# Running the first four attention slots inside the feed-forward stage of a two-layer transformer kernel

## The reference

```python
xn = _layernorm(x)
x = x + attn(xn, w_qkv, w_o) + ffn(xn, w_fc, w_proj)
# attn: 32 query heads, 4 key/value heads of 64, rotary embedding on q and k,
#       causal softmax over 256 keys, output projection from 2048 to 256
# ffn:  layer_norm, absmax quantisation (a straight-through value), ternary weights,
#       256 -> 1024, gelu, the same again, 1024 -> 256
```

## Time and profile before

| | us |
|---|---|
| median of 3 runs | 435.03 |
| lowest and highest run | 432.61, 436.24 |
| profiled execution | 434.22 |
| its span | 432.4 |
| PE busy | 394.3 (91%) |
| DVE busy | 359.2 (83%) |
| POOL busy | 279.6 (65%) |
| ACT busy | 264.0 (61%) |
| TensorE clock granted, mean | 0.976 |

### The profile page before, as it was taken

One profiled execution on the slowest core, in us unless ns is written; L12 is line 12 of the kernel. 1 busy time (PEld: TensorE's weight loads), 2 busy tenths in 40 slices (PEclk: granted clock), 3 DMA queues, 4 the chain that ended last, 5 costly groups with the idle time before them and its releaser, 6 DMA issues.

```text
span 432.4 us, 8674 instructions
## 1 busy us (share of the span) xinstructions
PE 394.3 (91%) x3002; PEld 362.9 (84%) x3002; DVE 359.2 (83%) x696; ACT 264.0 (61%) x818; POOL 279.6 (65%) x206
## 2 busy tenths in 40 slices
PE   3869796899978999999999989999998999999895
PEld 2556775699868999899999989999998999999785
DVE  3759699887738999889888987988998998899983
ACT  3350338877446667567666756766664676766671
POOL 6300152005879589986969998696998959697400
PEclk9977989999996999999999999999999999999999
DMA  7992040002453435543433554343346524324400
GB/s 230 375 349 72 0 181 15 2 1 50 108 130 81 99 76 130 133 98 72 107 92 85 131 130 122 74 104 93 90 115 145 133 48 116 86 64 113 106 2 24
DMA packets 39437, 45.20 MB, mean 105 GB/s; under 512 B 5601, under 2 KB 31970, under 8 KB 39138
## 3 DMA queue, kind: packets, MB, share of 16 engines
q1 hardware_dynamic: 39248, 44.65, 39.6%
q10 hardware_dynamic: 146, 0.00, 0.0%
HBM read 13.18 MB, written 1.05 MB: 33 GB/s over the span
## 4 chain that ended last, share of the span: by engine, by line
PE 43%; POOL 18%; DVE 17%; SPq 8%; issue 6%; ACT 4%; DMA 4%; POOLq 0%; ACTq 0%
PE bank L1273 7%; PE bank L1240 7%; PE bank L964 6%; PE bank L1291 6%; PE bank L1149 6%; DVE prob L916 5%; SPq L388 4%; POOL rope_a L627 4%; POOL split_hi L637 4%; POOL rope_a L638 4%; POOL rope_b L629 4%; POOL split_lo L639 3%; PE bank L1022 2%; DMA qT<-split_lo 2%; DVE neg_max L902 2%
## 5 line engine op out<-in xcount | busy, mean ns | idle before, releaser
L916 DVE TENSOR_TENSOR prob<-prob,rsum 128x512 f32<-128x512 f32 x96 | 112.5, 1172 | 3.3
L554 ACT ACTIVATE prob<-bank,neg_max 128x256 f32<-128x256 f32 (+1 forms) x256 | 104.6, 422 | 6.3 <-DVE neg_max L902 5.7
L564 ACT ACTIVATE probT_hi<-bank 128x512 fp32r<-128x512 f32 x96 | 57.5, 599 | 77.6 <-PE bank L964 77.6
L902 DVE TENSOR_REDUCE neg_max<-bank 128x2 f32<-128x512 f32 (+1 forms) x96 | 65.8, 685 | 27.1 <-PE bank L1243 26.0
L1240 PE MATMUL bank<-kT,qT 128*128 128x256 f32 (+1 forms) x512 | 75.5, 281 | 6.2 <-DMA qT<-split_lo 4.7
L1273 PE MATMUL bank<-probT_hi,v 128*128 128x256 f32 x384 | 76.9, 296 | 4.0 <-DVE oT_lo L928 3.9
L629 POOL TENSOR_TENSOR rope_b<-turned,cst 128x512 f32<-128x512 f32 x36 | 50.4, 1400 | 37.2 <-DMA turned<-raw 37.1
L1240 PEld LDWEIGHTS bank<-kT,qT 128*128 128x128 f32 x512 | 67.7, 195 | 7.6 <-DMA qT<-split_lo 5.7
L1273 PEld LDWEIGHTS bank<-probT_hi,v 128*128 128x128 f32 x384 | 59.0, 190 | 7.9 <-DVE probT_lo L922 7.0
L922 DVE TENSOR_TENSOR probT_lo<-bank,probT_hi 128x512 fp32r<-128x512 f32 x96 | 65.2, 679 | 0.2 <-ACT probT_hi L564 0.2
L964 PE MATMUL bank<-cst,prob 128*128 128x128 f32 x384 | 59.1, 277 | 2.5 <-DVE prob L916 2.5
(11 more groups left out here) (171 smaller groups left out, 802.0 us busy)
## 6 DMA issues: line engine op xcount, KB each, us to landing
turned<-raw SPq DMA_DIRECT2D x144, 64.0 KB, 2.0
qT<-split_hi SPq DMA_DIRECT2D x64, 128.0 KB, 2.4
qT<-split_lo SPq DMA_DIRECT2D x64, 128.0 KB, 2.4
nat_qkv<-in_L_attn_w_qkv_dram SPq DMA_DIRECT2D x1, 2560.0 KB, 22.8
wq<-in_L_attn_w_qkv_dram SPq DMA_DIRECT2D x4, 512.0 KB, 8.3
wout<-in_L_attn_w_out_dram SPq DMA_DIRECT2D x1, 2048.0 KB, 15.1
nat_o<-in_L_attn_w_o_dram SPq DMA_DIRECT2D x1, 2048.0 KB, 9.0
kT<-split_hi SPq DMA_DIRECT2D x16, 128.0 KB, 2.4
```

The lines of the kernel that those rows point to most:

```text
L554: ins = nc.scalar.activation(prob[n % 3][:, wide * j:wide * j + wide], bank[n % 2][:, wide * j:wide * j + wide], ACT.Exp, bias=neg_max[it ...
L902: dve.tensor_reduce(neg_max[n // UNITS % 2][:, unit_columns(n % UNITS)], bank[n % 2][:, :].rearrange("p (h k) -> p h k", h=heads), AX.X, A ...
L916: dve.tensor_tensor(a, a, share, ALU.mult).then_inc(s_norm, 1)
```

## The change

1. Slots 0, 1, 2 and 3 of the attention run at the ends of steps 8, 9, 10 and 11 on PE, ACT and DVE (`SLOTS_AT`). Slot 0 holds its fill, the second half of the queries of iteration 1. The load of the exponential's table follows `gelu(7)` in step 7.
2. The five fills move to steps 2 (k), 4 (q 0,0), 5 (q 0,1), 6 (v) and 7 (q 1,0). Shade units and fills share one list, `FILL`, and one pair of banks. The ring makes other columns of `qkvT` (8, 0, 1).
3. Waits: `scores(0)` for seven gelus, `prob_T(0)` for all eight, `prob_T(1)` for the last `hidden_lo`; the fills `v` and `q 1,0`, the first placing of queries and the clearing of `v` for all shade units.
4. Within the attention the next batch's keys are filled in u 5, behind the query block of that slot, in place of u 4.
5. POOL's order is changed to match; `v` is cleared in two parts in steps 5 to 8, only where nothing else writes, in place of two whole clears at the start. `w_o` is loaded right behind the other weights. Buffers move: `oT0`, `prob`, `probT_lo`, `nat_o`, `kT1`.

```diff
-RING_QKV = 3
+RING_QKV = (8, 0, 1)
...
             if u == 5 and it + 2 < ITS:
-                return [("q", it + 2, 0)]
+                return [("q", it + 2, 0)] + ([("k", b + 1)] if g == 1 and b + 1 < B else [])
             if u == 0 and it + 1 < ITS:
                 return [("q", it + 1, 1)]
-            if u == 4 and g == 1 and b + 1 < B:
-                return [("k", b + 1)]
...
-        PREPARE_STEPS = {5: [("k", 0)], 6: [("q", 0, 0)], 8: [("v", 0)], 9: [("q", 0, 1)], 11: [("q", 1, 0)]}
+        SPARE_EARLY = {2: [("qkvT", 5)], 3: [("woT", 0)], 4: [("woT", 3)], 5: [("woT", 6), ("woT", 7)]}
+        SPARE_LATE = {0: [("qkvT", 9), ("qkvT", 2)], 1: [("qkvT", 3), ("qkvT", 4)], 2: [("qkvT", 6), ("qkvT", 7), ("k", 0)],
+                      3: [("woT", 1), ("woT", 2)], 4: [("woT", 4), ("woT", 5), ("q", 0, 0)], 5: [("q", 0, 1)], 6: [("v", 0)],
+                      7: [("q", 1, 0)]}
+        SLOTS_AT = {8: (0,), 9: (1,), 10: (2,), 11: (3,)}
...
         def hidden_bank(t, half):
-            return bank[2 if half and t >= ALONE else 4]
+            return bank[3 if half and t >= ALONE else 4]
... (SP)
-            sp.wait_ge(filled, UNIT[("out0", B - 1)] + 1)
             sp.dma_start(nat_o[:, :, :], ...)
...
                     it, half = which
+                    if n < 2:
+                        sp.wait_ge(sh_done, len(SHADE))
... (ACT; DVE has the same shape)
+            for step in range(STEPS):
+                hidden_hi(step - 3, 0)
+                if 0 <= step - 2 < TILES:
+                    hidden_y(step - 2)
+                empty(SPARE_EARLY.get(step, ()))
...
+                hidden_hi(step - 3, 1)
+                if step < TILES:
+                    gelu(step)
+                if step == TILES - 1:
+                    nc.scalar.activation(table_use[:, 1:2], neg_magic[:, :], ACT.Exp)
...
+                empty(SPARE_LATE.get(step, ()))
+                for n in SLOTS_AT.get(step, ()):
+                    slot(n)
+            for n in range(sum(map(len, SLOTS_AT.values())), N_UNITS + 3):
+                slot(n)
... (POOL)
-            for par in range(2):
-                pool.memset(v[par][:, :].bitcast(F32), 0.0).then_inc(v_zero, 1)
...
+            def zero_values(par):
+                pool.wait_ge(sh_done, len(SHADE))
+                own = v[par][:, :].rearrange("p (n d) -> p n d", d=DH)[:, 0:33:2, :]
+                pool.memset(own.bitcast(F32), 0.0).then_inc(v_zero, 1)
-            for t in range(TILES - 2):
+            for t in range(3):
                 tile_root(t)
             rope_products(0)
-            tile_root(TILES - 2)
+            tile_root(3)
             rope_sums(0)
-            tile_root(TILES - 1)
-            for n in range(1, len(BLOCKS)):
+            tile_root(4)
+            rope_products(1)
+            tile_root(5)
+            zero_values(0)
+            rope_sums(1)
+            tile_root(6)
+            rope_products(2)
+            tile_root(7)
+            rope_sums(2)
+            zero_values(1)
+            for n in range(3, len(BLOCKS)):
... (PE)
                 elif n == 0:
-                    pe.wait_ge(f_gelu, TILES)
+                    pe.wait_ge(f_gelu, TILES - 1)
...
             def prob_T(n):
                 pe.wait_ge(s_norm, n + 1)
                 if n >= 2:
                     pe.wait_ge(t_lo, n - 1)
+                elif n == 0:
+                    pe.wait_ge(f_gelu, TILES)
+                else:
+                    pe.wait_ge(f_lo, 2 * TILES)
```

More of the change, by code:

```diff
@@ L569, in heads_hi, with slot @@
                 nc.scalar.activation(group_place(it, i)[0], group_bank(), ACT.Copy).then_inc(o_hi, 1)
[L571 to L573 removed]
+            def slot(n):
                 if 2 <= n < N_UNITS + 2:
@@ L945, in _ @@
                 if n < N_UNITS:
-                    new_values(fills_at(n // UNITS, n % UNITS))
+                    empty(fills_at(n // UNITS, n % UNITS))
                 if n % (HKV * UNITS) == UNITS - 1 and n >= HKV * UNITS:
                     add_out(n // (HKV * UNITS) - 1)
+            for step in range(STEPS):
+                t = step - 3
+                if 0 <= t < TILES:
+                    hidden_lo(t, 0)
+                if 1 <= step <= TILES:
+                    hidden_stats(step - 1)
+                if step == 0:
+                    ternary(nat_proj[:, :, :], winv[:, 2:3]).then_inc(tern_proj, 1)
+                if step == 1:
+                    y1_lo(2)
+                    y1_lo(3)
+                empty(SPARE_EARLY.get(step, ()))
+                if 0 <= t < TILES:
+                    hidden_lo(t, 1)
+                if 1 <= step <= TILES:
+                    hidden_factors(step - 1)
+                if t >= 1:
+                    ffn_add(t - 1)
+                empty(SPARE_LATE.get(step, ()))
+                for n in SLOTS_AT.get(step, ()):
+                    slot(n)
+            for n in range(sum(map(len, SLOTS_AT.values())), N_UNITS + 3):
+                slot(n)
             add_out(B - 1)
@@ L1166, in project_values, with shade_T @@
                 ins.then_inc(full[place], 1)
+            def shade_T(f):
+                place = next_place(f)
+                what, j = f
+                if what == "qkvT":
+                    blocks = [nat_qkv[:, c, P * k:P * k + P] for k in range(KC) for c in (2 * j, 2 * j + 1)]
+                else:
+                    pe.wait_ge(ld["o"], 16)
+                    blocks = [nat_o[:, k, P * c:P * c + P] for c in (2 * j, 2 * j + 1) for k in range(2)]
+                transposes(bank[place], blocks).then_inc(full[place], 1)
             def fill(fills):
                 for f in fills:
-                    if f[0] == "q":
+                    if f in SHADE:
+                        shade_T(f)
+                    elif f[0] == "q":
                         b, g = of_batch(f[1])
@@ L1294, in project_out, with slot @@
                     ins.then_inc(out_full, 1)
-            pe.wait_ge(const_done, 1)
-            for n in range(N_UNITS + 3):
+            def slot(n):
                 it, u = n // UNITS, n % UNITS
@@ L1308, in _ @@
                     project_out(it - 1, u // 3)
+            pe.wait_ge(const_done, 1)
+            for step in range(STEPS):
+                t = step - 3
+                if step == 1:
+                    pe.wait_ge(rel["dve"], released("dve", UNIT[("yT1", 1)]))
+                if t == 0:
+                    pe.wait_ge(proj_copied, FF // 256)
+                if 0 <= t < TILES:
+                    hidden_T(t, 0)
+                if step < TILES:
+                    fc(step)
+                fill(SPARE_EARLY.get(step, ()))
+                if step == 2:
+                    proj_T(0)
+                    proj_T(1)
+                if 0 <= t < TILES:
+                    hidden_T(t, 1)
+                if t >= 1:
+                    proj(t - 1)
+                if step == 1:
+                    y1_T(2)
+                    y1_T(3)
+                if step == 2:
+                    proj_T(2)
+                    proj_T(3)
+                fill(SPARE_LATE.get(step, ()))
+                for n in SLOTS_AT.get(step, ()):
+                    slot(n)
+            for n in range(sum(map(len, SLOTS_AT.values())), N_UNITS + 3):
+                slot(n)
             project_out(ITS - 1, 1)
```

190 lines of the change are left out of this document (61 added, 129 removed).

## The result

The changed kernel takes 438.65 us (median of 14 runs, 436.31 to 441.98) against 435.68 us for the kernel before (14 runs, 432.61 to 438.35, in turn on the same chip): a ratio of 1.0085, 95% interval 1.0057 to 1.0113. It is about 3 us slower; 429.6 was forecast, 5 us faster. The profiled execution took 437.48 us, its span 435.7.

The account below looks back on a forecast made before the run. PE bounds the kernel: its work, its idle time and its loss at the lower clock. Terms -7.6 + 2.35 + 1.1 - 0.9 = -5.0 us, from 434.6, give 429.6 us; range 425.5 to 434.0.

Parts of the forecast that it names:

- Boundary and slots (-7.6 + 2.35): Stage to attention, 115.2 to 139.9 us: overlap returns 7.6 us of idle and clock; slots under steps 8 to 11 add 2.35.
- the 3.0 us that the forecast put on the clock: At the boundary: 6.9 us at the low clock, PE busy about 5.9 of it, half of that lost.
- The early fills (+1.1): Steps 2 and 4 to 7: step 6 starts 4.0 us later, 2.9 of it moved work, so 1.1 new idle.
- scores(0) in time: End of step 8: first queries land at 112.8 us, scores(0) at 114.4, 1.6 us to spare, cost 0.
- The slower rival that I chose: End of step 8: scores(0) waits for its queries; one POOL block late gives 440.0 us; chance 0.10.
- The table load at nothing: Step 7 behind gelu(7): load takes 1.28 us, ACT through before hidden_hi(5,0) is wanted, cost 0.
- w_o earlier and the clears at nothing: Kernel start: w_o loaded earlier and clears of v removed there, cost taken as 0.
- The keys (-0.9): Attention, keys in u 5 behind the queries: 4.0 us of waits gained, 2.0 and 1.1 lost, net gain 0.9.
- The second half: Queries at u 3 of iterations 3, 7 and 11: 1.0, 0.7 and 0.4 us late, 2.0 together.
- Slot 5 with two fills, and slot 4 with none: u 4 without its fill: 0.37 us of wait for oT_lo, three more such waits, 1.1 us.
- a fall of the clock past 60 us: Sign of being wrong: the clock row showing a 0.5 anywhere past 60 us.
- the key block costs more than it frees: Rival, attention: second half 2.5 us late three times, keys +4.6 instead of -0.9, 435.1 us, no difference; chance 0.11.

Follow-up runs that it names:

- keys_alone: The kernel before with only the next keys filled in u 5 behind the query block: 441.60 us (6 runs), ratio 1.0183.
- before_u2: The kernel before with only the key block moved to slot 2 of the second iteration instead of slot 4: 432.87 us (10 runs), ratio 0.9938.
- no_slots: The changed kernel with keys in slot 4 again and slots 0 to 3 behind the stage, early fills kept: 434.19 us (12 runs), ratio 0.9968.
- keys_back: The changed kernel with the next keys filled in slot 4 again: 432.17 us (12 runs), ratio 0.9942.
- place_first: The changed kernel, keys still in slot 5, SP placing the second half of the queries ahead of the next block's swap: 444.28 us, ratio 1.0195.
- keys_g0u2: The changed kernel with the keys in slot 2 of the first iteration of a batch: 435.98 us (12 runs), ratio 1.0008.
- fill_order: keys_back with the fills of steps 2 and 4 put between two weight units: 428.79 us (6 runs), ratio 0.9841.
- keys_u2: The changed kernel with the keys in slot 2 of the second iteration: 429.88 us (9 runs), ratio 0.9907.

## Why the prediction was wrong, by its steps

In the profiled execution the forecast was -5.0 us and the outcome +3.3. The 8.3 us between are: the keys 6.2, the early fills 1.0, the start 1.0 (scatter), the rest under 0.2.

- **Boundary and slots (-7.6 + 2.35): the sum came out, one of its terms did not.** From `fc(1)` to iteration 0, u 5 the changed kernel gained 3.0 us net. The early fills cost 2.1 of idle (next point), so the rest gained 5.1, forecast 5.25. The clock stayed up. But this holds against the one trace that the forecast was read from. In keys_alone and before_u2 the same boundary kept its clock and was 1.3 us shorter, so the 3.0 us that the forecast put on the clock were mis-sized and are not lost every time; against those two the changed start gains 1.7 us net. That the sum agreed so well is luck in part. The idle pieces came at other places than laid out: none ahead of `proj(7)`, but 0.84 us for `hidden_y(7)` on ACT, which I had not listed. What the forecast didn't separate is the slots' own share: by no_slots it is about 2 us (not clear of noise), and the rest came with the other parts of the change or with the clock.
- **The early fills (+1.1), too small.** `fc(6)` starts 38.31 us after `fc(1)`, before 33.35: 4.96 us later, of which 2.9 is moved work, so 2.1 of new idle. The place was right (the key fill behind `qkvT_lo`, 2.00 us; step 3's wait kept, 0.93; the query fill's, 0.98). By the forecast's own pieces the new idle was 77.7 - 75.8 = 1.9 for the key fill, instead of 0.78 before, and 0.8 for the query fill: 1.9 in all. I booked 1.1, from where I had let step 6 start, and the pieces were right. What the clock may lose behind such a wait, 1.24 us in keys_back and place_first, was not priced.
- **scores(0) in time, right.** Its queries' last placing was issued at 112.62 us; with the page's 2.4 us to landing that is 115.0, and `scores(0)` started at 116.53: 1.5 us to spare, forecast 1.6. The slower rival that I chose was the wrong one.
- **The table load at nothing, right.** In the changed kernel it took 1.28 us at 112.37, as in the earlier trace rows, and nothing on PE waited for `hidden_hi(5,0)` at 114.44. From the end of the gelu to ACT's next copy there are 1.60 us, the first small use included. The 2.66 us that the Trainium skill, page "ScalarE: Activation LUTs", section "What ACT_TABLE_LOAD costs", gives for a switch were not seen here; the measurement decides.
- **w_o earlier and the clears at nothing, right** as far as the traces tell: `fc(1)` moved no further than it scatters. A cost below 1 us isn't excluded: the nine traces with the new start have it at 62.61 to 64.46 us, the three with the old one at 62.42, 62.54 and 63.62.
- **The keys (-0.9): this is the step that failed.** Its first part holds: the waits in u 0 of iterations 3, 7 and 11 are gone, all 4.0 us. The rest was mis-sized on every term. The second half was forecast 1.0, 0.7 and 0.4 us late; it was 2.19, 1.53 and 1.33. The next second half, in iterations 4 and 12, was late as well (0.45 and 0.52), which the sum had not. Slot 5 with two fills, and slot 4 with none, cost 2.5 us over the three batches by the starts of the maxima (2.9 by what is left of the sum below) where 1.1 was forecast. And the clock fell once behind the wait of 2.19, 1.7 us. Together -4.0 + 6.0 + 2.9 + 1.7 = +6.6 from iteration 1 to 12; 1.4 came back in the last iterations, 1.2 in keys_back too. The forecast had named a fall of the clock past 60 us as a sign of being wrong, and it was there.

Why the half was so late shows in SP's queue of the changed kernel, from the last of the keys' placings to the half's:

```profile
180.31 1.27 SPq L390 DMA_DIRECT2D kT<-split_lo  x2
181.68 0.57 SPq L366 DMA_DIRECT2D turned<-raw  x1
182.29 1.99 SPq L367 DMA_DIRECT2D turned<-raw  x1
184.32 0.59 SPq L366 DMA_DIRECT2D turned<-raw  x1
184.96 0.59 SPq L367 DMA_DIRECT2D turned<-raw  x1
185.65 0.65 SPq L387 DMA_DIRECT2D qT<-split_hi  x1
...
187.68 0.62 SPq L387 DMA_DIRECT2D qT<-split_lo  x1
```

POOL and PE of the same kernel:

```profile
181.82 1.62 POOL L637 TENSOR_TENSOR split_lo<-rope_a,split_hi 128x512 fp32r<-128x512 f32 x1
```
```profile
190.42 1.56 PE L1230 MATMUL bank<-kT,qT 128*128 128x128 f32 x8 [2.19 <-DMA qT<-split_lo]
```

POOL was done with the half at 183.4, 1.2 us earlier than forecast, so SP's queue made it late. SP's last placing went out at 187.68, 0.33 later than forecast: the queue was 1.3 us ahead of the forecast when the keys were placed, and lost that when one swap DMA took 1.99 us to issue. It landed 2.7 us later, not 2.35. And PE wanted it at 188.23, not 188.7, because the changed kernel stood 1.64 us ahead of the kernel before at that point, where the forecast had allowed 1.0, the wait in u 0. Each size was off by less than 0.5 us, all three in the same direction, and at 2.2 us of wait the clock went too.

The slow issue is no accident of this batch. In the other two there is one as well in the swap between the keys and the half:

```profile
261.90 1.26 SPq L367 DMA_DIRECT2D turned<-raw  x1
339.66 1.41 SPq L367 DMA_DIRECT2D turned<-raw  x1
```

SP went on to the half's placings without a pause each time, with POOL long done. So, as an estimate, with all three at their neighbours' 0.59 us the waits would have been 0.8, 0.9 and 0.5 us, and the forecast had 1.0, 0.7 and 0.4. keys_alone has such an issue at the same place in all three batches too (1.56, 1.00 and 1.70 us). The term that the sum left out is thus the slow issue, some 3 us of lateness in all, though the forecast had named it as what spoke for its rival.

That rival, "the key block costs more than it frees", had this mechanism, a half 2.5 us late, with a chance of 0.11. It had 1.1 us for the slots without a fill and nothing for the clock. With the 1.8 us more that slot 5 cost and one fall of the clock (1.7) its 435.1 would have been about 438.6, slower, and it should have been the slower rival.

## What to carry to other kernels

- A queue that runs several blocks back to back (here POOL, 7.45 us a block, two blocks in every iteration and a third in some) has little room for an extra block, and its place decides how long the engine behind it waits: PE's waits for queries were 6.0 us in all with the keys in slot 5, 4.3 in slot 4, 2.1 in slot 2, and 5.8 in slot 2 an iteration earlier. Ask of every place by how much the block behind it misses its slot. Here slot 2 or 3 ahead of the pair was best, slot 5 inside the pair worst by some 9 us.
- Price a wait of about 2 us at up to twice its length where the clock may fall behind it, and don't book a fall seen in one trace as a sure gain. Count slow issues into a long chain of DMAs, and add up lateness with the errors of each term in the bad direction before a small net gain is booked.
- When a list of work shares banks in rotation, check which item last had the bank. Exchanging neighbours in two steps gave 3.4 us by the medians (2.0 of them idle time of PE), more than the overlap of the stages.

## What the runs showed of the hardware that was not expected

- The clock does not fall behind every wait of that size. It fell behind 2.19 us (changed kernel), two of three waits of 2.1 us and one of 2.00 (place_first), 2.52 us (keys_g0u2), 2.00 us (keys_back), and 1.74 and 1.67 us (keys_alone). It stayed at 1.00 behind 2.09 us (place_first), 1.97 and 2.00 us (keys_g0u2), 2.13 us (fill_order), 2.00 us (changed kernel) and 1.99 us (keys_u2).
- Most DMA issues on SP take 0.57 to 0.65 us. Of the 308 in each trace from 60 us on, 5 to 16 take about 1 us or more, up to 2.2. The chain of sixteen from the keys' first placing to the half's last held one in all six cases (changed kernel and keys_alone); why is not known.
- DVE's small casts run several times longer beside a clear on POOL, in all three traces that have the clear and in none of the other nine. The timeline of DVE in the kernel before, where POOL clears `v` from 3.29 us on the earlier trace rows, and then in the changed one, where those clears are gone:

```profile
3.50 1.74 DVE L694 CAST ident_b<-cst 128x128 bf16<-128x128 f32 x1 [2.65 <-DMA cst<-const_dram]
3.64 3.73 DVE L696 CAST mask_b<-cst 128x128 bf16<-128x128 f32 x4
```
```profile
3.48 0.23 DVE L707 CAST ident_b<-cst 128x128 bf16<-128x128 f32 x1 [2.61 <-DMA cst<-const_dram]
3.62 0.63 DVE L709 CAST mask_b<-cst 128x128 bf16<-128x128 f32 x4
```

The casts take 0.86 us in place of 5.47. It gives no time here, since DVE then waits for x either way.
